# Attention scores in four 32-row strips with accumulation in PSUM, and the shift as the exponential's bias

## What is computed

```python
H, hd = 16, 32
q, k, v = (heads(x @ W.T) for W in (Wq, Wk, Wv))            # 4 x 16 x 2048 x 32 each
attn = softmax(einsum('nhqd,nhkd->nhqk', q, k) / sqrt(hd), axis=3)
x = layernorm(x + merge_heads(einsum('nhql,nhld->nhqd', attn, v)))
w = (ffn_weights >= 0) * 2 - 1
x = layernorm(x + clip((x @ w.T) * scale + bias, -100, 100))
```

## Time and profile before

| | |
|---|---|
| median of three runs | 2922.89 us |
| the profiled execution, first to last instruction | 2917.2 us |
| granted TensorE clock, mean share of full speed | 0.985 |
| PE busy | 2785.6 us (95%) |
| DVE busy | 2319.8 us (80%) |
| ACT busy | 2300.0 us (79%) |
| GpSimd busy | 343.1 us (12%) |

### The profile page before, as it was taken

One profiled execution on the slowest core, in us unless ns is written; L12 is line 12 of the kernel. 1 busy time (PEld: TensorE's weight loads), 2 busy tenths in 40 slices (PEclk: granted clock), 3 DMA queues, 4 the chain that ended last, 5 costly groups with the idle time before them and its releaser, 6 DMA issues.

```text
span 2917.2 us, 79173 instructions
## 1 busy us (share of the span) xinstructions
PE 2785.6 (95%) x29276; PEld 1423.5 (49%) x29276; DVE 2319.8 (80%) x2050; ACT 2300.0 (79%) x2789; POOL 343.1 (12%) x342
## 2 busy tenths in 40 slices
PE   8999999979999999999999999999999999997998
PEld 7888888833333333333333333344343333335887
DVE  4334343469898898989889899898989989897998
ACT  3333333379999999999999999999999999894665
POOL 0000000010000000000000000000000000004665
PEclk9999999989999999999999999999999999998999
DMA  5544445556675766767576675767667576655553
GB/s 190 182 179 173 173 173 180 182 134 144 143 160 117 166 130 140 154 138 153 119 168 128 141 164 123 160 121 162 137 142 167 117 161 134 132 122 182 187 206 130
DMA packets 223563, 445.69 MB, mean 153 GB/s; under 512 B 15442, under 2 KB 130130, under 8 KB 198868
## 3 DMA queue, kind: packets, MB, share of 16 engines
q0 software_dynamic: 27504, 200.29, 35.6%
q1 hardware_dynamic: 186596, 224.71, 24.7%
q10 hardware_dynamic: 9216, 16.78, 1.5%
HBM read 123.47 MB, written 117.96 MB: 83 GB/s over the span
## 4 chain that ended last, share of the span: by engine, by line
PE 73%; issue 4%; ACT 2%; DVE 1%; POOL 0%; ACTq 0%; DMA 0%; SPq 0%; DVEq 0%; POOLq 0%
PE banks L637 33%; PE banks L666 30%; PE banks L1008 6%; PE banks L683 2%; ACT probs L764 1%; PE banks L997 1%; PE banks L990 1%; PE banks L1004 1%; ACT L764 0%; POOL score_rows L587 0%; PE banks L991 0%; DVE partial L821 0%; ACT y L1026 0%; DVE stats L1071 0%; DVE score_rows L773 0%
## 5 line engine op out<-in xcount | busy, mean ns | idle before, releaser
L764 ACT ACTIVATE probs<-banks 128x1024 f32<-128x1024 f32 x2048 | 1891.9, 1149 | 99.6 <-PE banks L637 95.3
L637 PE MATMUL banks<-score_rows 97*32 97x512 f16 x16384 | 1186.8, 384 | 90.1 <-issue 65.8
L666 PE MATMUL banks<-probs,v_keys 128*32 128x512 f32 x8192 | 1094.5, 598 | 3.4 <-issue 3.1
L637 PEld LDWEIGHTS banks<-score_rows 97*32 97x32 f16 x16384 | 431.6, 95 | 1076.1 <-ACT probs L764 578.0
L821 DVE TENSOR_TENSOR partial<-partial,probs 128x2048 f32<-128x2048 f32 x384 | 879.7, 2291 | 50.0 <-ACT probs L764 37.7
L818 DVE TENSOR_TENSOR partial<-probs 128x2048 f32<-128x2048 f32 x192 | 440.2, 2293 | 78.6 <-ACT probs L764 74.0
L606 POOL DMA_DIRECT2D total<-partial x191 | 164.9, 863 | 1847.8 <-DVE partial L821 865.5
L666 PEld LDWEIGHTS banks<-probs,v_keys 128*32 128x32 f32 x8192 | 287.3, 112 | 181.3 <-issue 9.5
L821 DVE TENSOR_TENSOR total<-total,probs 128x2048 f32<-128x2048 f32 x128 | 292.7, 2287 | 2.6
L348 DVE TENSOR_TENSOR qk_lo<-banks,qk_hi 128x512 f16<-128x512 f32 x128 | 88.5, 692 | 240.8 <-ACT qk_hi L292 240.8
L292 ACT ACTIVATE qk_hi<-banks 128x512 f16<-128x512 f32 x128 | 76.4, 597 | 234.2 <-PE banks L246 234.2
(11 more groups left out here) (94 smaller groups left out, 2164.1 us busy)
## 6 DMA issues: line engine op xcount, KB each, us to landing
total<-partial POOLq DMA_DIRECT2D x191, 1024.0 KB, 8.2
x_in<-in_L_attn_x SPq DMA_DIRECT2D x17, 1024.0 KB, 7.3
scratch_q_raw<-qk_raw SPq DMA_DIRECT2D x16, 1024.0 KB, 5.5
scratch_k_raw<-qk_raw SPq DMA_DIRECT2D x16, 1024.0 KB, 5.6
scratch_v<-v_out SPq DMA_DIRECT2D x16, 1024.0 KB, 5.0
score_rows<-scratch_q_hi SPq DMA_DIRECT2D x128, 128.0 KB, 6.4
score_rows<-scratch_k_hi SPq DMA_DIRECT2D x128, 128.0 KB, 3.8
v_keys<-scratch_v SPq DMA_DIRECT2D x64, 256.0 KB, 6.9
```

What stands on the lines that cost most here:

```text
L637: last = nc.tensor.matmul(scores_of(unit)[part, i, :], k_rows[:, h, keys], q_rows[:, h, qb * BLK:(qb + 1) * BLK], start=True, stop=True)
L666: last = nc.tensor.matmul(banks[rows, out_bank(qb), :], v_keys[:, kt, rows], probs[:, kt % P_RING, h, :], start=(kt == 0), stop=(kt == KT ...
L764: nc.scalar.activation(probs[:, kt % P_RING, heads, :], scores_of(qb * UNITS + u), ACT.Exp, scale=SCALE / GAIN ** 2).then_inc(a_prob, 1)
```

## The change

The 97-row layout goes. `rows16` now holds four arrays of 128 partitions: q_hi, q_lo, k_hi, k_lo, each with the four heads' 32 rows in the four 32-row strips, by 2048 columns. A tile's scores are 12 matmuls: for each of the three products (k_hi q_hi, k_hi q_lo, k_lo q_hi) the four heads, each with 32 rows and 128 weight columns, each to its own bank, accumulated over the three products. The two units of a tile share one wait, the one that the second had, ahead of the first matmul; both are counted in the last product. The shift row, its fill and DVE's write go; the shift is scaled to be the exponential's bias, a pointer to a 128 x 1 tile, and ACT waits once for it. Loads of q and k are 2 instead of 3 per 512 columns. The exact way gets a `q_exact` of its own and a shift of zero.

```diff
-    rows16 = sb("score_rows", [P, 2, G, S], FP16)
-    q_rows, k_rows = rows16[0:KROWS, 0], rows16[0:KROWS, 1]
+    rows16 = sb("score_rows", [P, 4, S], FP16)
+    q_hi, q_lo, k_hi, k_lo = (rows16[:, i] for i in range(4))
+    terms = ((k_hi, q_hi), (k_hi, q_lo), (k_lo, q_hi))
...
-            for r, part in enumerate(("q_hi", "q_lo", "q_hi")):
-                src = dram[part].rearrange("n (g h r) t -> (n g) r h t", g=NG, r=HD)[bass.ds(it, 1), :, :, cols]
-                sp.dma_start(q_rows[HD * r:HD * r + HD, :, cols], src.rearrange("o r h t -> (o r) h t")).then_inc(a_q[c], 16)
+            for part, dst in (("q_hi", q_hi), ("q_lo", q_lo)):
+                src = dram[part].rearrange("n (g p) t -> (n g) p t", g=NG)[bass.ds(it, 1), :, cols]
+                sp.dma_start(dst[:, cols], src.rearrange("o p t -> (o p) t")).then_inc(a_q[c], 16)
...
-        nc.gpsimd.memset(k_rows[3 * HD:KROWS], K_SHIFT).then_inc(a_const, 1)
-        pool.wait_ge(a_const, 1)
...
-            for half in range(2):
-                unit = qb * UNITS + 2 * kt + half
-
-                pe.wait_ge(a_prob, it * ITEM_UNITS + slot_before(unit) + 1 + SLOTS)
-                for i in range(2):
-                    h = 2 * half + i
-                    for c in range(G):
-                        part = slice(HD * c, HD * c + HD)
-                        keys = slice(kt * P + HD * c, kt * P + HD * c + HD)
-                        last = nc.tensor.matmul(scores_of(unit)[part, i, :], k_rows[:, h, keys],
-                                                q_rows[:, h, qb * BLK:(qb + 1) * BLK], start=True, stop=True)
-                last.then_inc(a_score, 1)
+            unit = qb * UNITS + 2 * kt
+            keys = slice(kt * P, (kt + 1) * P)
+            cols = slice(qb * BLK, (qb + 1) * BLK)
+
+            pe.wait_ge(a_prob, it * ITEM_UNITS + slot_before(unit + 1) + 1 + SLOTS)
+            for i, (k_part, q_part) in enumerate(terms):
+                for h in range(G):
+                    rows = slice(HD * h, HD * h + HD)
+                    last = nc.tensor.matmul(scores_of(unit + h // 2)[:, h % 2, :], k_part[rows, keys], q_part[rows, cols],
+                                            start=(i == 0), stop=(i == 2))
+                    if i == 2 and h % 2 == 1:
+                        last.then_inc(a_score, 1)
...
-            pe.wait_ge(a_const, 2)
-            pe.wait_ge(a_shift, 1)
+            pe.wait_ge(a_const, 1)
             all_items(fast_scores)
...
         nc.scalar.activation(wf_hi[:], wf_scaled[:], ACT.Copy).then_inc(a_wfhi, 1)
+        act.wait_ge(a_shift, 1)
...
                     nc.scalar.activation(probs[:, kt % P_RING, heads, :], scores_of(qb * UNITS + u), ACT.Exp,
-                                         scale=SCALE / GAIN ** 2).then_inc(a_prob, 1)
+                                         scale=SCALE / GAIN ** 2, bias=shift[:]).then_inc(a_prob, 1)
...
-        dve.wait_ge(a_const, 1)
-        nc.vector.tensor_scalar(q_rows[3 * HD:KROWS], k_rows[3 * HD:KROWS], 0.0, shift[3 * HD:KROWS], ALU.mult, ALU.add).then_inc(a_shift, 1)
```

More of the change, by code:

```diff
@@ L41 @@
 MAX_VAL = 100.0
-KROWS = 3 * HD + 1
 GAIN = 1024.0
-K_SHIFT = 32768.0
 SHIFT = 0.25
@@ L369, in _ @@
         dve.wait_ge(s_bound, 1)
-        nc.vector.tensor_scalar(shift[:], bound[:], -SHIFT / K_SHIFT, None, ALU.mult).then_inc(s_top, 1)
+        nc.vector.tensor_scalar(shift[:], bound[:], -SHIFT * SCALE / GAIN ** 2, None, ALU.mult).then_inc(s_top, 1)
         for c in range(DC):
@@ L387, in sem @@
         return ctx.enter_context(nc.semaphore(name))
-    rows16 = sb("score_rows", [P, 2, G, S], FP16)
-    q_rows, k_rows = rows16[0:KROWS, 0], rows16[0:KROWS, 1]
-    rows32 = rows16[:].bitcast(FP32)
-    q_exact = rows32[0:HD + 1, 0, :, 0:BLK]
-    k_exact = rows32[0:HD + 1, 1]
+    rows16 = sb("score_rows", [P, 4, S], FP16)
+    q_hi, q_lo, k_hi, k_lo = (rows16[:, i] for i in range(4))
+    terms = ((k_hi, q_hi), (k_hi, q_lo), (k_lo, q_hi))
+    q_exact = sb("q_exact", [HD + 1, G, BLK], FP32)
+    k_exact = rows16[:].bitcast(FP32)[0:HD + 1]
     v_keys = sb("v_keys", [P, KT, P], FP32)
@@ L434, in attend @@
     m_ones = sem("m_ones")
+    m_zero = sem("m_zero")
     m_q = sem("m_q")
@@ L441, in attend @@
     HEAD = DEN_TILE + 1
-    FIRST_Q = 48
-    FIRST_K = 48
+    FIRST_Q = 32
+    FIRST_K = 32
     def scores_of(unit):
@@ L464, in load_q @@
             cols = slice(c * BLK, (c + 1) * BLK)
-            for r, part in enumerate(("q_hi", "q_lo", "q_hi")):
-                src = dram[part].rearrange("n (g h r) t -> (n g) r h t", g=NG, r=HD)[bass.ds(it, 1), :, :, cols]
-                sp.dma_start(q_rows[HD * r:HD * r + HD, :, cols], src.rearrange("o r h t -> (o r) h t")).then_inc(a_q[c], 16)
+            for part, dst in (("q_hi", q_hi), ("q_lo", q_lo)):
+                src = dram[part].rearrange("n (g p) t -> (n g) p t", g=NG)[bass.ds(it, 1), :, cols]
+                sp.dma_start(dst[:, cols], src.rearrange("o p t -> (o p) t")).then_inc(a_q[c], 16)
         def load_k(it, c):
             cols = slice(c * BLK, (c + 1) * BLK)
-            for r, part in enumerate(("k_hi", "k_hi", "k_lo")):
-                src = dram[part].rearrange("n (g h r) t -> (n g) r h t", g=NG, r=HD)[bass.ds(it, 1), :, :, cols]
-                sp.dma_start(k_rows[HD * r:HD * r + HD, :, cols], src.rearrange("o r h t -> (o r) h t")).then_inc(a_k[c], 16)
+            for part, dst in (("k_hi", k_hi), ("k_lo", k_lo)):
+                src = dram[part].rearrange("n (g p) t -> (n g) p t", g=NG)[bass.ds(it, 1), :, cols]
+                sp.dma_start(dst[:, cols], src.rearrange("o p t -> (o p) t")).then_inc(a_k[c], 16)
         def load_v(n, g, c):
@@ L493, in finish_stores @@
             sp.dma_start(attn_first[:], dram["attn"][0, :, 0:BLK].rearrange("(c p) t -> p c t", p=P)).then_inc(first_in, 16)
-            sp.wait_ge(a_const, 6)
+            sp.wait_ge(a_const, 2)
             sp.dma_start(den_first[0:H, :], dram["den"][0:H, 0:BLK]).then_inc(first_in, 16)
@@ L593, in _ @@
                                 pattern=[[-1, P]], channel_multiplier=1).then_inc(m_id, 1)
-        pool.wait_ge(a_const, 2)
-        nc.gpsimd.memset(first[1][:], 0.0).then_inc(a_const, 4)
+        pool.wait_ge(a_const, 1)
+        nc.gpsimd.memset(first[1][:], 0.0).then_inc(a_const, 1)
         pool.sem_inc(m_max, 2)
@@ L783, in _ @@
             nc.vector.memset(k_exact[HD:HD + 1], 1.0).then_inc(m_ones, 1)
+            nc.vector.memset(shift[:], 0.0).then_inc(m_zero, 1)
+            dve.wait_ge(m_zero, 1)
             with dve.Fori(0, N * H) as h:
@@ L791, in _ @@
                 nc.vector.tensor_scalar(max_neg[:], banks[0:KT, 0, 0:P], -1.0, None, ALU.mult).then_inc(m_neg, 1)
+        dve.sem_inc(a_shift, 1)
         def copy_out(st, parity):
```

## The result

The changed kernel takes 3233.64 us (median of four runs, 3230.56 to 3236.32) against 2922.22 for the kernel before beside it: 1.1064 times as long, 95% interval 1.1049 to 1.1080. That is 311 us slower. 3390 had been forecast, with a range of 3080 to 3520.

A forecast was written before the change was run, and what follows sets the result against it. ACT's exponentials were taken to bound the kernel, a tile-to-tile loop after the change. Attention 2391 + 20.5 table loads + 70 stalls = 2481.5 against 2011.5, start -2.5: span 3384.7, plus 5.7 around it: 3390 us; range 3080 to 3520.

The forecast's parts named there:

- turn: Attention, tile to tile: exponential, wait, three score passes, next exponential, all in series; 2.31 us a tile against 1.84 before.
- first pass: First four of a tile's score matmuls on PE, behind the wait: 0.33 us with tiling change and exposed weight load.
- rival B: New fp16 weights of 128 columns load in no extra time: passes 0.22, loop 2.20, kernel 3280 us; chance 0.10.
- A: The tile-to-tile loop in attention as summed: kernel 3390 us; chance 0.58.
- change of tiling back: On PE between a tile's scores and its values: 0.11 us for changing the array's tiling.
- Rival E: Strips fail: weights load one after another, 4170 us, chance 0.10; or matmuls go one by one, over 5500, chance 0.03.
- Rival C: Each score pass exposes its weight loads, the second 0.33 too: loop 2.41, kernel 3490 us; chance 0.08.
- Denominators: Once a query block PE adds 0.87 us of denominator work, ending 0.42 past the gate.
- Stalls: PE's instruction stalls in attention: 90 us before, 30 to 110 after, 70 taken.
- Rival F: PE idles, so its clock drops to the half level (1.2 GHz): 3.2 us a tile, 4300 us; chance 0.02.
- Rival D: The loop costs nothing beyond ACT's own work, as the wait is met early: 3090 us; chance 0.05.
- Rival G: Pointer free and third pass early enough, so ACT stays the bound at 1.84 us a tile: 2816 us; chance 0.03.

The follow-up runs named there:

- kernel with own waits: The changed kernel, pointer kept, with its strips in four staggered passes and a separate wait for each unit: 3127.41 us, 1.0709.
- combined one: The kernel before without the shift row, with ACT's wait for scores last and four items per turn of ACT's loop: 2908.03 us, 0.9953.

## Why the prediction was right, and where its size was off

The sign, the mechanism and the range held. The forecast was 156 us too high. Its loop against the traces, us per turn:

| step | forecast | measured |
|---|---|---|
| exponential with pointer | 1.12 | 1.11 |
| its end to the weight load | 0.05 | 0.05 |
| first pass | 0.33 | 0.23 |
| second pass | 0.23 | 0.22 |
| third pass, start to end | 0.39 | 0.37 |
| its end to the exponential | 0.19 | 0.18 |
| turn | 2.31 | 2.16 to 2.17 |

- **The mis-sized term is the first pass.** 0.10 of the 0.145 a turn, so 102 of the 148 us that the loop accounts for. The forecast had put a change of tiling and a cold weight load there from the earlier trace rows, whose weights are fp32. The new ones, 128 columns of fp16, load in 93 ns where 128 of fp32 take 188 (group rows above), and of the change of tiling nothing shows behind the gate. The value of rival B, a turn of 2.20 and 3280 in all, is nearest; it had been given 0.10, and A 0.58. The Trainium skill, "TensorE: Matmul & The Clock Gate", section on weight-path modes, says that 128-column weights that are not fp32 load about twice as fast. The trace agrees (93 against 188 ns), but the two rows differ in type and in rows (32 against 128), and no run takes these apart.
- **The change of tiling back** to the values, put at 0.11, was right: in PE's timeline a tile's scores start at 735.44 and its values at 736.20, 0.76 later, where three passes at 0.22 to 0.23 would be 0.67.

```profile
735.44 0.83 PE L633 MATMUL banks<-score_rows 32*128 32x512 f16 x12 [0.34 <-ACT probs L761]
736.20 1.06 PE L663 MATMUL banks<-probs,v_keys 128*32 128x512 f32 x8
...
749.88 0.83 PE L633 MATMUL banks<-score_rows 32*128 32x512 f16 x12 [1.35 <-ACT probs L761]
```

- **The pointer** at 0.09: 1.113 against 1.02 to 1.03 without, 0.09 less a turn when it was taken out. The Trainium skill, "ScalarE: Activation LUTs", section "What ACT_TABLE_LOAD costs", gives about 93 ns for such an operand; 0.087 was measured in a queue and 0.09 in the loop.
- **Strips** run four side by side: the passes are 0.22 apart. Rival E is out. Rival C is out too: the eight weight loads of the first two passes are done at 1501.57, while the first pass, on the same rows, runs until 1501.86. The Trainium skill, "TensorE: Matmul & The Clock Gate", section on packing, has the rule that loads overlap only matmuls of other row groups; it doesn't hold here.
- **Denominators**: 0.49 idle a block, 0.45 beyond what a turn idles anyway, against 0.42 forecast.
- **Stalls**: 2330.8 - 2246 - 20.5 = 64 against 70, but not of the parts that were thought of. ACT waits 14 times for 2.71 to 4.61 behind a stop of PE, and seven times for about 1.0 in the tile after; beyond what a turn and the denominators idle anyway that is some 46. Another 15 us are a term that the forecast had missed: at an item's end the wait is met one exponential later (the 1.35 of idle time at 749.88 above, against 0.34). 128 units over three slots don't come out even, so an item's units 0 and 1 take the slots of the last two, and the joint wait then asks for the very last exponential: 1.0 us, at 15 item ends. Behind some of the stops PE also runs on the lower clock: behind a stop of 2.37 us the 2.2 us from 782.30 on have a granted clock of 1.00, and behind one of 2.33 the 3.4 us from 927.44 on have 0.51. The first scores then take 1.47 us instead of 0.83, and ACT's wait is 3.52 instead of 2.93:

```profile
927.44 1.47 PE L633 MATMUL banks<-score_rows 32*128 32x512 f16 x12 [2.33 <-issue]
```

- **Start**: the first exponential came 3.4 us earlier (607.0 for 610.4), 2.5 forecast. What the start alone is worth in the kernel before is nothing, as its run showed, because the stage gave it back. Whether the changed kernel kept its own wasn't tried.
- **What lies around the span**: 3.1 us, not 5.7.
- **Clock**: 1.00 in steady work, 0.83 around a stop, mean 0.987. Rival F is out: in the steady loop PE idles 0.34 a tile and keeps the upper level (2.4 GHz).
- Rival D (ACT's own work sets the pace) is what the kernel with own waits came to, not the change: there 32 exponentials run without a gap. Rival G needed a free pointer and a third pass that ends within 0.57 us of the gate; the pointer costs 0.09, and the pass ended 0.83 after PE's first weight load behind it.
- **The signs** named in the forecast: exponentials of 1.11, PE's idle time ahead of each tile's scores and ACT as what ends it were right. ACT's own figures were not. Its wait ahead of a pair is 2.165 - 2.12 = 0.04, not about 0.3, because the turn is shorter and a pair lasts 1.11 + 1.01 = 2.12; and its busy time is 2170.7 / 2048 = 1.06 per exponential, not 1.01, because only the second of a pair overlaps another.
- **Slips in the working**: 0.22 x 1024 is 225, not 221, and 2068 is 176 above 1892, not 184. Neither enters the sum of the forecast.

The same sum gave four other turns before their runs: 2.07, 1.86, 2.29 and 1.95, measured 2.075, 1.88, 2.30 and 1.94. For the kernel with own waits it gave 1.95, below ACT's own 2.01, and 2.009 was measured. It sizes a loop to within 0.02 us when its terms come from rows of the same instructions. The whole times of these kernels were missed by 8 to 47 us, largely because PE's stops, which the sum doesn't hold, changed from kernel to kernel.

## What to carry to other kernels

Where a buffer's release and its refill wait for each other, add up the one serial loop (the consumer's instruction, the wait, the producer until its first result is ready, the wait) and compare it with each engine's own work; less work on an engine that waits in the loop is worth only what it shortens there. A producer that finishes several buffers together lengthens that loop by all its passes but the first buffer's (370 us here), and one wait for two buffers does it again: interleave for speed only as far as the first buffer's completion stays early. On the engine that sets the pace put the wait that ends last behind the others, and no pointer where a constant or another engine can do it.

## What the runs showed that had not been expected

- Three waits on ACT, of which the first ended last, cost 0.13 us more than with that one behind the others (turn 2.075 to 1.94), for the same instructions.
- A pointer as the bias of a 128 x 1024 exponential costs 0.087 us also where the exponentials queue, but only 0.054 in the time of the whole kernel before (111 us for 2048), since idle time on ACT fell by 60.
- PE's stops where its loop closes depend on what surrounds them. Three items in the loop's body instead of one took 45 us from the changed kernel and 28 from the combined one, with the same matmuls. What they are stays open.
- Gains ahead of or beside the stage were given back in it: 5 us of an earlier start and 15 us of table loads changed the total by nothing that could be measured.
